# Three of sixteen states of a selective scan get their input product on GpSimd, and TensorE adds the skip term

## The chip, the cores and the metric

The kernel runs on one core of one Trainium2 chip. The metric is the device time of one execution in microseconds. The engines are TensorE (PE, matmuls), VectorE (DVE), ScalarE (ACT), GpSimd (POOL) and SyncE (SP, here only DMAs). Each takes its own instructions in the order in which they are written, and they meet through semaphores.

## The reference

Four layers run one after the other on x of 2 x 2048 x 128: an RWKV block, a feed-forward block of ternary weights, a selective state-space layer and a mixture of eight experts. The change touches only the state-space layer. For a batch row, with inner width 256 and 16 states, it computes

```
h, gate = split(xn @ W_in);  h = silu(causal_conv(h));  gate = silu(gate)
ts, Bm, Cm = split(h @ W_x);  dt = softplus(ts @ W_dt + b_dt)
state[t] = exp(dt[t] * -exp(A_log)) * state[t-1] + dt[t] * h[t] * Bm[t]     (256 x 16 states)
y[t] = sum over the 16 states of state[t] * Cm[t]   +   D * h[t]
out = layer_norm((y * gate) @ W_out);   x = x + out
```

The code folds a layer norm in front of this layer into `xn`.

## The kernel before, in words

The stage is `phase_ssm`. Channels lie on the 128 partitions, so the width 256 makes CB = 2 chunks, and time lies along the free dimension in tiles of N = 512 columns. Two batch rows by NT = 4 stretches of time give eight tiles, taken one after the other; the text calls them the first to the eighth (or last). The tiles of t = 1 and t = 2 are the third to the sixth. A tile works through DST = 16 states, numbered n = 0 to 15, and `body` of each engine is written as a loop over n.

For a state n:

- TensorE broadcasts the row of B over the partitions (L990, into a bank of `pD`) and the row of C (L993, into `pC`).
- ScalarE copies C to SBUF (`csb`, L1103) and computes the decay exp(dt * A) of the next state for both chunks (`dA`, L1092).
- VectorE multiplies `dtu` = dt * h with the broadcast of B. This product is called dBu. For an odd n it is two instructions (L1252, L1253), for an even n one of 1024 columns (L1255). Its result lies in `pD` in PSUM. Then it runs the recurrence with one TENSOR_TENSOR_SCAN for each chunk (L1240).
- GpSimd multiplies the scanned state with C for both chunks (`prod`, L1177) and keeps the last column as carry (L1168).
- TensorE sums the products of all states with an identity matrix in `pY` (`accumulate`, L979), LAG = 3 states behind: in iteration n it takes state n-3, and in n = 0, 1, 2 the last three states of the tile before.

`dA`, `hs`, `csb` and `prod` are rings of four slots.

Into this loop the work of the neighbouring tiles is written. `prep` prepares the next tile: TensorE has a step of it in each iteration n = 0 to 9 (centring, variance, four convolution steps L931 in n = 2 to 5, gate projection L938 in n = 6, the projections to ts, B and C L945 in n = 7 and 8, dt L952 in n = 9). ScalarE has its steps in n = 0, 1, 4, 5, 6, 8, 9, 10 and 11 (L1051 parks the convolution in n = 4 and 5; in n = 6 come two table loads, the silu of h and of the gate; L1062 and L1065 copy ts and `split` in n = 8). VectorE has xn in n = 1 (L1208), L1212, L1216 and L1219 in n = 8, 9 and 10. `tail` finishes the tile before: VectorE adds D * h to `pY` in n = 2 (L1225) and frees `pY` with it, GpSimd multiplies with the gate (L1160), TensorE projects down in n = 11 and takes a variance in n = 13. The first product of a tile, `accumulate(t, b, 0)` in n = 3, has to wait until that VectorE tail has read `pY`. ScalarE and GpSimd also split two pieces of expert weights in each of the first six tiles, which SyncE loads into two buffers `raw`.

## Time and profile before

| | us |
|---|---|
| median of 3 runs (lowest, highest) | 1486.36 (1486.03, 1488.72) |
| the profiled execution, its own time | 1486.03 |
| its span, first to last instruction | 1483.9 |
| mean granted clock of TensorE | 0.905 of full speed |

The scan stage fills the slices 17 to 31 of the 40 on the page. The page gives busy time in tenths of each slice, and the clock that TensorE was granted:

```profile
PE   4444279969789698797978888797866837978864
DVE  3676544644644453389999999999998286755644
ACT  2555343442443433575858677685743623544544
POOL 0111232230330220268788787878776246777773
PEclk8677589989999998999999999999999957999995
```

VectorE is at 9 tenths through the stage, the others at 6 to 9.

In a timeline row the first number is the start in us from the span's start and the second the duration of the whole group (xCOUNT). Matmuls in f32 of 512 columns are recorded as two MATMULs each, so a pair over two chunks is x4. PE ends are modelled and overlap the next start; the distance of two starts is the rate. What stands in brackets is the engine's idle time before the row and what ended it.

### The profile page before, as it was taken

How to read it: one execution, taken by the hardware profiler on the slowest of the kernel's cores; microseconds unless marked ns; L12 is line 12 of the kernel's file. 1: busy time of each engine (PE TensorE's matmuls, PEld its weight loads, DVE VectorE, ACT ScalarE, POOL GpSimd, SP SyncE). 2: the span in 40 equal slices, each digit the busy share in tenths (PEclk: the TensorE clock that was granted, in tenths of full speed). 3: DMA queues.
4: the chain of work that ended last, by engine and by line, in shares of the span. 5: the costliest groups of instructions: out<-in, count | busy, mean ns of one | idle time of the engine just before them, and what ended most of it. 6: DMA issues, size and time to landing. Idle time of an engine off the chain costs nothing. (4 is left out here: it accounts for less than half of the span.)

```text
span 1483.9 us, 16813 instructions
## 1 busy us (share of the span) xinstructions
PE 1110.5 (75%) x4986; PEld 549.9 (37%) x4986; DVE 1008.9 (68%) x1422; ACT 767.9 (52%) x1248; POOL 738.6 (50%) x615
## 2 busy tenths in 40 slices
PE   4444279969789698797978888797866837978864
PEld 1111123424334244232333333333322425967753
DVE  3676544644644453389999999999998286755644
ACT  2555343442443433575858677685743623544544
POOL 0111232230330220268788787878776246777773
PEclk8677589989999998999999999999999957999995
DMA  6000000000000000000000000000000001111124
GB/s 200 0 0 0 0 0 1 1 1 1 0 0 0 0 0 29 0 29 0 29 0 29 14 15 17 12 0 0 0 1 0 29 29 37 50 51 50 50 50 169
DMA packets 13842, 33.17 MB, mean 22 GB/s; under 512 B 3568, under 2 KB 3760, under 8 KB 13552
## 3 DMA queue, kind: packets, MB, share of 16 engines
q1 hardware_dynamic: 8784, 22.10, 4.5%
q0 software_dynamic: 4992, 10.23, 2.4%
q8 instruction: 36, 0.59, 0.2%
q14 instruction: 30, 0.25, 0.1%
HBM read 23.01 MB, written 9.31 MB: 22 GB/s over the span
## 5 line engine op out<-in xcount | busy, mean ns | idle before, releaser
L1177 POOL TENSOR_TENSOR prod<-hs,csb 128x1024 f32<-128x1024 f32 x128 | 303.9, 2375 | 117.7 <-DVE hs L1240 115.2
L1240 DVE TENSOR_TENSOR_SCAN hs<-dA,carry,pD 128x512 f32<-128x512 f32 x256 | 313.8, 1267 | 5.5 <-DVE pD L1255 0.8
L979 PE MATMUL pY<-prod,const 128*128 128x512 f32 x512 | 244.8, 600 | 11.6 <-DVE h L1225 7.4
L1092 ACT ACTIVATE dA<-dt,negA 128x512 f32<-128x512 f32 x256 | 169.3, 712 | 2.5 <-POOL dt L1149 2.5
L1103 ACT ACTIVATE csb<-pC 128x512 f32<-128x512 f32 x128 | 76.2, 595 | 154.8 <-PE pC L993 154.6
L979 PEld LDWEIGHTS pY<-prod,const 128*128 128x128 f32 x512 | 95.3, 190 | 120.9 <-issue 98.5
L645 ACT ACTIVATE stage<-pR,vec 128x512 f32<-128x512 f32 x64 | 44.0, 687 | 123.7 <-PE pR L481 123.7
L1914 DVE SCALAR_TENSOR_TENSOR hid<-pR,silu 128x512 f32<-128x512 f32 x78 | 53.9, 691 | 65.7 <-ACT silu L1646 65.6
L1699 POOL DMA_INDIRECT g<-moe_rows,source x78 | 81.9, 1050 | 26.9 <-issue 23.2
L1255 DVE TENSOR_TENSOR pD<-dtu,pD 128x1024 f32<-128x1024 f32 x64 | 78.5, 1227 | 22.6 <-POOL dtu L1153 9.9
L1715 POOL DMA_INDIRECT moe_outs<-y,to x78 | 80.9, 1038 | 23.8 <-issue 23.2
L990 PE MATMUL pD<-split,sel 96*128 96x512 bf16 x128 | 50.2, 392 | 54.1 <-DVE hs L1240 54.1
L1646 ACT ACTIVATE silu<-pR 128x512 f32<-128x512 f32 x78 | 46.6, 597 | 81.5 <-PE pR L1439 81.5
L1437 PE MATMUL pR<-x,moe_hi 128*128 128x256 f16 x312 | 87.3, 280 | 0.9 <-DVE x L1898 0.9
L1438 PE MATMUL pR<-x,moe_hi 128*128 128x256 f16 x312 | 87.2, 279 | 0.0
L1439 PE MATMUL pR<-x,moe_lo 128*128 128x256 f16 x312 | 87.0, 279 | 0.0
L666 POOL TENSOR_TENSOR mix_lo<-mix,mix_hi 128x512 f16<-128x512 f32 x8 | 9.5, 1210 | 152.3 <-DVE mix_hi L730 152.3
L931 PE MATMUL pQ<-xn,convw 128*128 128x512 f32 x128 | 67.2, 654 | 17.9 <-DVE xn L1208 17.8
L301 POOL TENSOR_TENSOR o<-o,rs 128x512 f32<-128x512 f32 x8 | 11.7, 1464 | 136.1 <-DVE o L394 136.1
L705 DVE TENSOR_SCALAR B_hi<-stage 128x512 f16<-128x512 f32 x64 | 36.9, 582 | 51.9 <-ACT stage L645 51.9
L705 DVE TENSOR_SCALAR A_hi<-stage 128x512 f16<-128x512 f32 x64 | 28.0, 442 | 46.0 <-ACT stage L645 46.0
L1545 PE MATMUL pY<-moe_hi,hid_hi 128*128 x312 | 57.3, 221 | 0.8 <-DVE hid_lo L1905 0.8
(342 smaller groups left out, 2776.1 us busy)
## 6 DMA issues: line engine op xcount, KB each, us to landing
raw<-moe_w SPq DMA_DIRECT2D x12, 512.0 KB, 3.6
room<-moe_outs SPq DMA_DIRECT2D x8, 512.0 KB, 8.5
X<-xT SPq DMA_DIRECT2D x4, 512.0 KB, 4.5
hidw<-hid_w SPq DMA_DIRECT2D x1, 2048.0 KB, 10.1
moe_rows<-xt SPq DMA_DIRECT2D x8, 256.0 KB, 2.0
outT<-X SPq DMA_DIRECT2D x8, 256.0 KB, 2.0
g<-moe_rows,source POOLq DMA_INDIRECT x78, 2.8
moe_outs<-y,to POOLq DMA_INDIRECT x78, 2.5
```

The lines of the kernel that those rows point to most:

```text
L931: last = nc.tensor.matmul(Q[c][:], convw[:, c, k, :], xn[:, b, k:k + N], start=k == 0, stop=k == TAPS - 1)
L979: last = nc.tensor.matmul(YB[c][:], G.ident, prod[:, slot(b, n), c, :], start=n == 0, stop=n == DST - 1)
L1092: last = nc.scalar.activation(dA[:, slot(b, n), c, :], dt[:, b, c, :], ACT.Exp, scale=negA[:, c, n:n + 1])
L1103: nc.scalar.activation(csb[:, slot(b, n), 0, :], CC[:], ACT.Copy).then_inc(S["c_in"], 1)
L1177: nc.gpsimd.tensor_tensor(prod[:, slot(b, n), :, :], hs[:, slot(b, n), :, :], csb[:, slot(b, n), :, :].to_broadcast([P, CB, N]), ALU.mult)\
L1240: last = nc.vector.tensor_tensor_scan(hs[:, slot(b, n), c, :], dA[:, slot(b, n), c, :], dBu(n, c), carry[:, b, n, c:c + 1], ALU.mult, ALU.add)
L1255: last = nc.vector.tensor_tensor(DD[:, 0:CB, :], dtu[:, b, :, :], bcastB(n).unsqueeze(1).to_broadcast([P, CB, N]), ALU.mult)
L1437: nc.tensor.matmul(out, w_hi, x_hi, start=start, stop=False)
L1438: nc.tensor.matmul(out, w_hi, x_lo, start=False, stop=False)
L1439: return nc.tensor.matmul(out, w_lo, x_hi, start=False, stop=stop)
L1699: nc.gpsimd.indirect_dma_start(g[:, i % GR, r, :], None, rows, bass.IndirectOffsetOnAxis(ap=source[:, 2 * i + r:2 * i + r + 1], axis=0))\
L1715: nc.gpsimd.indirect_dma_start(outs, bass.IndirectOffsetOnAxis(ap=to[:, 2 * i + r:2 * i + r + 1], axis=0), y[:, i % YR, r, :], None).then_ ...
```

## The change

HELPED names the states 3, 5 and 9. For these, VectorE no longer makes dBu. Three iterations ahead (LEAD), TensorE broadcasts their row of B into `pC` behind the broadcast of C, ScalarE copies it to SBUF (`bsb`), and GpSimd multiplies `dtu` with it into `helped` (two buffers). Their decay goes to the banks of `pD` in PSUM that their dBu would have filled (`decay_helped`); the half in the first bank waits until the scan of the state before has read it (`scan0`). Their scans take chunk 1 first.

D * h is added by TensorE, with a diagonal matrix of D, into the sum in `pY` in n = 10; VectorE's tail then multiplies the sum with the gate itself, and GpSimd's gate multiplication is gone.

On TensorE, the broadcast of B for state n+1 stands in iteration n, behind `accumulate(n-3)` and ahead of `prep`; before it stood at the head of iteration n+1. With it, `accumulate` has moved ahead of `prep`.

To make room in SBUF, `raw` and `scaled` have one buffer instead of two. The core of the diff:

```
+    HELPED = (3, 5, 9)
+    OWN = tuple(n for n in range(DST) if n not in HELPED)
+    LEAD = 3
...
+        bsb = sb("bsb3", [P, 1, N])
+
+        diagD = G.win[:, 0:INTER].rearrange("p (c m) -> p c m", c=CB)
+        helped = sb("helped3", [P, 2, CB, N])
         prod = sb("prod3", [P, RING, CB, N])
...
-        raw = sb("raw3", [P, 2, 2 * FFN])
+        raw = sb("raw3", [P, 2 * FFN])
...
+        def before_helped(n):
+
+            i = HELPED.index(n)
+            return HELPED[i - 2] + 1 if i >= 2 else HELPED[i - 2] + 1 - DST
...
-                if i >= 2:
-                    sp.wait_ge(S["w_low"], i - 1)
-                sp.dma_start(raw[:, i % 2, :], G.moe_w13[:, i, :] if i < E else w2[:, i - E, :])\
-                  .then_inc(S[f"w_in{i % 2}"], 16)
+                if i >= 1:
+                    sp.wait_ge(S["w_low"], i)
+                sp.dma_start(raw[:, :], G.moe_w13[:, i, :] if i < E else w2[:, i - E, :])\
+                  .then_inc(S["w_in"], 16)
...
-                    wait_past(pe, S["y"], chunk(t, b, 0) - 1)
+                    wait_past(pe, S["ygated"], at(t, b) - 1)
...
+            def broadcast_b(t, b, n):
+                wait_past(pe, S["scan"], state(t, b, n) - 2)
+                nc.tensor.matmul(bcastB(n), G.sel[:, n, :], split[:, b, :], start=True, stop=True)\
+                  .then_inc(S["bcastB"], 1)
+
             def body(t, b):
                 for n in range(DST):
 
                     if n == 0:
                         pe.wait_ge(S["split3"], at(t, b))
                         pe.wait_ge(S["split4"], at(t, b))
-                    wait_past(pe, S["scan"], state(t, b, n) - 2)
-                    nc.tensor.matmul(bcastB(n), G.sel[:, n, :], split[:, b, :], start=True, stop=True)\
-                      .then_inc(S["bcastB"], 1)
+                        broadcast_b(t, b, 0)
                     wait_past(pe, S["c_in"], state(t, b, n) - 1)
+                    if n - 1 + LEAD in HELPED:
+                        pe.wait_ge(S["b_in"], among(t, b, n - 1 + LEAD, HELPED))
                     nc.tensor.matmul(CC[:], G.sel[:, DST + n, :], split[:, b, :],
                                      start=True, stop=True).then_inc(S["bcastC"], 1)
+                    if n + LEAD in HELPED:
+                        pe.wait_ge(S["c_in"], state(t, b, n))
+                        nc.tensor.matmul(CC[:], G.sel[:, n + LEAD, :], split[:, b, :], start=True, stop=True)\
+                          .then_inc(S["bcastH"], 1)
                     if n < LAG and not is_first(t, b):
                         accumulate(*before(t, b), DST - LAG + n)
+                    if n >= LAG:
+                        accumulate(t, b, n - LAG)
+                    if n + 1 in OWN:
+                        broadcast_b(t, b, n + 1)
                     if not is_last(t, b) and n in PE_PREP:
                         prep(*after(t, b), PE_PREP.index(n))
                     if not is_first(t, b) and n in PE_TAIL:
                         tail(*before(t, b), PE_TAIL.index(n))
-                    if n >= LAG:
-                        accumulate(t, b, n - LAG)
+                    if n == 10:
+                        for c in range(CB):
+                            nc.tensor.matmul(YB[c][:], diagD[:, c, :], h[:, b, c, :], start=False, stop=False)
...
+            pe.wait_ge(S["diagD"], 1)
...
+            def decay_helped(t, b, n):
+                act.wait_ge(S["scan"], state(t, b, n) - 2)
+                nc.scalar.activation(dBu(n, 1), dt[:, b, 1, :], ACT.Exp, scale=negA[:, 1, n:n + 1])
+                act.wait_ge(S["scan0"], among(t, b, n, HELPED))
+                nc.scalar.activation(dBu(n, 0), dt[:, b, 0, :], ACT.Exp, scale=negA[:, 0, n:n + 1])\
+                  .then_inc(S["dA"], 1)
+
             def body(t, b):
                 for n in range(DST):
                     if n == 0:
                         act.wait_ge(S["dt"], at(t, b))
                         decay(t, b, 0)
+                    if n in HELPED:
+                        decay_helped(t, b, n)
                     act.wait_ge(S["bcastC"], state(t, b, n))
                     wait_past(act, S["prod"], slot_before(t, b, n))
                     nc.scalar.activation(csb[:, slot(b, n), 0, :], CC[:], ACT.Copy).then_inc(S["c_in"], 1)
-                    if n + 1 < DST:
+                    if n + LEAD in HELPED:
+                        act.wait_ge(S["bcastH"], among(t, b, n + LEAD, HELPED))
+                        wait_past(act, S["dBuH"], among(t, b, n + LEAD, HELPED) - 1)
+                        nc.scalar.activation(bsb[:, 0, :], CC[:], ACT.Copy).then_inc(S["b_in"], 1)
+                    if n + 1 in OWN:
...
-                    pool.wait_ge(S["y"], chunk(t, b, CB - 1))
-                    wait_past(pool, S["down"], at(t, b) - 1)
-                    nc.gpsimd.tensor_tensor(ygate[:, :, :], h[:, b, :, :], sgate[:, b, :, :], ALU.mult)\
-                      .then_inc(S["ygated"], 1)
-                elif step == 1:
                     pool.wait_ge(S["scaledC"], at(t, b))
-                    nc.gpsimd.tensor_tensor(X[:, b, ds(t)], X[:, b, ds(t)], scaled[:, b, :], ALU.add)\
+                    nc.gpsimd.tensor_tensor(X[:, b, ds(t)], X[:, b, ds(t)], scaled[:, :], ALU.add)\
...
+                    if n + LEAD in HELPED:
+                        k = among(t, b, n + LEAD, HELPED)
+                        pool.wait_ge(S["b_in"], k)
+                        wait_past(pool, S["scan"], state(t, b, 0) - 1 + before_helped(n + LEAD))
+                        nc.gpsimd.tensor_tensor(helped[:, HELPED.index(n + LEAD) % 2, :, :], dtu[:, b, :, :],
+                                                bsb[:, :, :].to_broadcast([P, CB, N]), ALU.mult)\
+                          .then_inc(S["dBuH"], 1)
                     if not is_last(t, b) and n in (10, 11, 12):
                         prep(*after(t, b), (10, 11, 12).index(n))
-                    if not is_first(t, b) and n in (2, 15):
-                        tail(*before(t, b), (2, 15).index(n))
+                    if not is_first(t, b) and n == 15:
+                        tail(*before(t, b), 0)
...
             def tail(t, b, step):
                 if step == 0:
                     dve.wait_ge(S["acc"], state(t, b, DST - 1))
+                    wait_past(dve, S["down"], at(t, b) - 1)
                     for c in range(CB):
-                        nc.vector.scalar_tensor_tensor(out=h[:, b, c, :], in0=h[:, b, c, :], scalar=col("D", c),
-                                                       in1=YB[c][:], op0=ALU.mult, op1=ALU.add).then_inc(S["y"], 1)
+                        last = nc.vector.tensor_tensor(ygate[:, c, :], YB[c][:], sgate[:, b, c, :], ALU.mult)
+                    last.then_inc(S["ygated"], 1)
                 elif step == 1:
                     dve.wait_ge(S["rstdC"], at(t, b))
-                    wait_past(dve, S["addedC"], at(t, b) - B)
-                    nc.vector.tensor_tensor(scaled[:, b, :], Q[0][:], rstd[:, b, :], ALU.mult)\
+                    wait_past(dve, S["addedC"], at(t, b) - 1)
+                    nc.vector.tensor_tensor(scaled[:, :], Q[0][:], rstd[:, b, :], ALU.mult)\
                       .then_inc(S["scaledC"], 1)
...
             def scan(t, b, n):
-                dve.wait_ge(S["dBu"], state(t, b, n))
-                dve.wait_ge(S["dA"], state(t, b, n))
-
                 wait_past(dve, S["prod"], slot_before(t, b, n))
                 wait_past(dve, S["kept"], slot_before(t, b, n))
-                for c in range(CB):
-                    last = nc.vector.tensor_tensor_scan(hs[:, slot(b, n), c, :], dA[:, slot(b, n), c, :],
-                                                        dBu(n, c), carry[:, b, n, c:c + 1],
-                                                        ALU.mult, ALU.add)
+                dve.wait_ge(S["dA"], state(t, b, n))
+                if n in OWN:
+                    dve.wait_ge(S["dBu"], among(t, b, n, OWN))
+                    for c in range(CB):
+                        last = nc.vector.tensor_tensor_scan(hs[:, slot(b, n), c, :], dA[:, slot(b, n), c, :],
+                                                            dBu(n, c), carry[:, b, n, c:c + 1],
+                                                            ALU.mult, ALU.add)
+                        if c == 0 and n + 1 in HELPED:
+                            last.then_inc(S["scan0"], 1)
+                else:
+                    dve.wait_ge(S["dBuH"], among(t, b, n, HELPED))
+                    for c in (1, 0):
+                        last = nc.vector.tensor_tensor_scan(hs[:, slot(b, n), c, :], dBu(n, c),
+                                                            helped[:, HELPED.index(n) % 2, c, :],
+                                                            carry[:, b, n, c:c + 1], ALU.mult, ALU.add)
                 last.then_inc(S["scan"], 1)
 
             def body(t, b):
                 for n in range(DST):
                     if n == 0:
                         dve.wait_ge(S["dtu"], at(t, b))
-                    dve.wait_ge(S["bcastB"], state(t, b, n))
-                    wait_past(dve, S["scan"], state(t, b, n) - 1)
-                    if n % 2:
+                    if n in HELPED:
+                        pass
+                    elif n % 2:
+                        dve.wait_ge(S["bcastB"], among(t, b, n, OWN))
+                        wait_past(dve, S["scan"], state(t, b, n) - 1)
                         nc.vector.tensor_tensor(dBu(n, 0), dtu[:, b, 0, :], bcastB(n), ALU.mult)
-                        last = nc.vector.tensor_tensor(dBu(n, 1), dtu[:, b, 1, :], bcastB(n), ALU.mult)
+                        nc.vector.tensor_tensor(dBu(n, 1), dtu[:, b, 1, :], bcastB(n), ALU.mult).then_inc(S["dBu"], 1)
                     else:
-                        last = nc.vector.tensor_tensor(DD[:, 0:CB, :], dtu[:, b, :, :],
-                                                       bcastB(n).unsqueeze(1).to_broadcast([P, CB, N]), ALU.mult)
-                    last.then_inc(S["dBu"], 1)
+                        dve.wait_ge(S["bcastB"], among(t, b, n, OWN))
+                        wait_past(dve, S["scan"], state(t, b, n) - 1)
+                        nc.vector.tensor_tensor(DD[:, 0:CB, :], dtu[:, b, :, :],
+                                                bcastB(n).unsqueeze(1).to_broadcast([P, CB, N]), ALU.mult)\
+                          .then_inc(S["dBu"], 1)
...
+            dve.wait_ge(S["turned"], 1)
+            for c in range(CB):
+                last = nc.vector.tensor_scalar(diagD[:, c, :], G.ident, col("D", c), None, ALU.mult)
+            last.then_inc(S["diagD"], 1)
```

TensorE from iteration n = 3 on in a middle tile, before (L990 B, L993 C, L931 convolution for the next tile, L979 sum):

```order
L990 MATMUL pD<-split,sel 128x512
L993 MATMUL pC<-split,sel 128x512
L931 MATMUL pQ_0<-xn,convw 128x512 x2
L979 MATMUL pY_0<-prod,const 128x512
L979 MATMUL pY_1<-prod,const 128x512
L990 MATMUL pD<-split,sel 128x512
L993 MATMUL pC<-split,sel 128x512
L931 MATMUL pQ_1<-xn,convw 128x512 x2
L979 MATMUL pY_0<-prod,const 128x512
L979 MATMUL pY_1<-prod,const 128x512
```

And in the changed kernel from the same place (L1014 C, L995 sum, L1001 B of the next state, L947 convolution):

```order
L1014 MATMUL pC<-split,sel 128x512
L995 MATMUL pY_0<-prod,const 128x512
L995 MATMUL pY_1<-prod,const 128x512
L1001 MATMUL pD<-split,sel 128x512
L947 MATMUL pQ_0<-xn,convw 128x512 x2
L1014 MATMUL pC<-split,sel 128x512
L995 MATMUL pY_0<-prod,const 128x512
L995 MATMUL pY_1<-prod,const 128x512
L947 MATMUL pQ_1<-xn,convw 128x512 x2
L1014 MATMUL pC<-split,sel 128x512
L995 MATMUL pY_0<-prod,const 128x512
L995 MATMUL pY_1<-prod,const 128x512
```

The convolution of iteration 3 stood ahead of the first sum of the tile and now stands behind it; iterations 4 and 5 have lost or moved their broadcast of B.

TensorE in iteration n = 6 of the changed kernel (L1018 is the broadcast of B for a helped state, L954 the gate projection):

```order
L1014 MATMUL pC<-split,sel 128x512
L1018 MATMUL pC<-split,sel 128x512
L995 MATMUL pY_0<-prod,const 128x512
L995 MATMUL pY_1<-prod,const 128x512
L1001 MATMUL pD<-split,sel 128x512
L954 MATMUL pQ_0<-xn,ssmw 128x512
L954 MATMUL pQ_1<-xn,ssmw 128x512
```

Two broadcasts now go to the one tile `pC` in a row; between them lies ScalarE's copy of the first.

ScalarE in iterations 8 and 9, before (L1103 csb, L1092 decays, L1062 ts, L1065 split):

```order
L1103 ACTIVATE csb<-pC 128x512
L1092 ACTIVATE dA<-dt,negA 128x512 x2
L1062 ACTIVATE tsb<-pQ_0 64x512
L1065 ACTIVATE split<-pQ_1 96x512
L1103 ACTIVATE csb<-pC 128x512
L1092 ACTIVATE dA<-dt,negA 128x512 x2
```

And in the changed kernel (L1144 csb, L1093 ts, L1096 split, L1130 and L1132 the decay of helped state 9, L1124 decays of state 10):

```order
L1144 ACTIVATE csb<-pC 128x512
L1093 ACTIVATE tsb<-pQ_0 64x512
L1096 ACTIVATE split<-pQ_1 96x512
L1130 ACTIVATE pD<-dt,negA 128x512
L1132 ACTIVATE pD<-dt,negA 128x512
L1144 ACTIVATE csb<-pC 128x512
L1124 ACTIVATE dA<-dt,negA 128x512 x2
```

The decays of state 9 stood ahead of the copies of ts and split, and now stand behind them.

## Rows read from the trace of the kernel before

**Rows 1.** The page, costliest groups: busy us, mean ns, idle before

```profile
L1177 POOL TENSOR_TENSOR prod<-hs,csb 128x1024 f32<-128x1024 f32 x128 | 303.9, 2375 | 117.7 <-DVE hs L1240 115.2
...
L1240 DVE TENSOR_TENSOR_SCAN hs<-dA,carry,pD 128x512 f32<-128x512 f32 x256 | 313.8, 1267 | 5.5 <-DVE pD L1255 0.8
...
L979 PE MATMUL pY<-prod,const 128*128 128x512 f32 x512 | 244.8, 600 | 11.6 <-DVE h L1225 7.4
```

**Rows 2.** Busy time by stretch, tail to tail, six middle tiles

```profile
core 0: us, PE busy (x) PEld busy (x) DVE busy (x) ACT busy (x) POOL busy (x), PEclk, DMA share, GB/s
...
765.06:830.34 65.28, 54.92 (x139) 22.13 (x138) 63.09 (x65) 46.89 (x74) 53.38 (x39) 1.00 0.05 17
...
sum 393.68, PE 330.30 PEld 131.79 DVE 377.72 ACT 276.94 POOL 315.94; mean PE 55.05 PEld 21.97 DVE 62.95 ACT 46.16 POOL 52.66
```

**Rows 3.** Waits of VectorE there: us, times, longest

```profile
DVE pD L1255 <- PE pD L990: 5.3, 7, 1.2
```

**Rows 4.** Timeline, VectorE, third tile: start us, us

```profile
762.69 2.45 DVE L1240 TENSOR_TENSOR_SCAN hs<-dA,carry,pD 128x512 f32<-128x512 f32 x2 [0.19 <-DVE pD L1255]
765.06 1.38 DVE L1225 SCALAR_TENSOR_TENSOR h<-h,vec,pY 128x512 f32<-128x512 f32 x2
...
774.05 0.70 DVE L1252 TENSOR_TENSOR pD<-dtu,pD 128x512 f32<-128x512 f32 x1
...
775.38 2.45 DVE L1240 TENSOR_TENSOR_SCAN hs<-dA,carry,pD 128x512 f32<-128x512 f32 x2
777.94 1.23 DVE L1255 TENSOR_TENSOR pD<-dtu,pD 128x1024 f32<-128x1024 f32 x1
...
794.02 0.76 DVE L1216 CAST mid<-sq 96x512 bf16<-96x512 f32 x1
```

**Rows 5.** Timeline, TensorE in the third tile

```profile
763.68 1.88 PE L931 MATMUL pQ<-xn,convw 128*128 128x512 f32 x4
...
766.58 1.96 PE L979 MATMUL pY<-prod,const 128*128 128x512 f32 x4 [1.02 <-DVE h L1225]
768.37 0.38 PE L990 MATMUL pD<-split,sel 96*128 96x512 bf16 x1
768.59 0.38 PE L993 MATMUL pC<-split,sel 96*128 96x512 bf16 x1
768.81 1.88 PE L931 MATMUL pQ<-xn,convw 128*128 128x512 f32 x4
770.53 1.88 PE L979 MATMUL pY<-prod,const 128*128 128x512 f32 x4
...
786.13 1.88 PE L945 MATMUL pQ<-h,ssmw 128*96 128x512 f32 x4
```

**Rows 6.** Timeline, ScalarE in the third tile

```profile
769.01 0.60 ACT L1103 ACTIVATE csb<-pC 128x512 f32<-128x512 f32 x1 [3.32 <-PE pC L993]
769.50 1.32 ACT L1092 ACTIVATE dA<-dt,negA 128x512 f32<-128x512 f32 x2
...
789.00 0.58 ACT L1065 ACTIVATE split<-pQ 96x512 bf16<-96x512 f32 x1
```

**Rows 7.** Timeline, TensorE in other tiles, after waiting

```profile
695.22 3.66 PE L931 MATMUL pQ<-xn,convw 128*128 128x512 f32 x4 [2.35 <-DVE xn L1208]
...
1024.17 1.99 PE L931 MATMUL pQ<-xn,convw 128*128 128x512 f32 x4 [2.34 <-DVE xn L1208]
...
1093.91 3.75 PE L979 MATMUL pY<-prod,const 128*128 128x512 f32 x4 [4.60 <-DVE h L1225]
```

**Rows 8.** Timeline, TensorE and VectorE in the first tile

```profile
632.91 0.63 PE L993 MATMUL pC<-split,sel 96*128 96x512 bf16 x1
...
662.72 0.75 DVE L1216 CAST mid<-sq 96x512 bf16<-96x512 f32 x1
```

**Rows 9.** Timeline, the end of the stage

```profile
1150.61 2.34 POOL L1160 TENSOR_TENSOR ygate<-h,sgate 128x1024 f32<-128x1024 f32 x1 [2.21 <-DVE h L1225]
...
1153.10 1.95 PE L960 MATMUL pQ<-ygate,ssmw 128*128 128x512 f32 x4 [1.84 <-POOL ygate L1160]
```

24 lines of the change are left out of this document (13 added, 11 removed).

## The prediction

> **What bounds the kernel now.** I read the page first, for where the change lies and what is full there. VectorE is busiest in the scan stage; its largest group is the scans, 256 of 1267 ns, almost without idle time before them, while GpSimd's products wait for those scans for 115.2 us [rows 1]. Then the busy time from tail to tail (start of the L1225 pair) of the six middle tiles: a tile takes 65.6 us (393.68 / 6), in which VectorE is busy 62.95, GpSimd 52.7, ScalarE 46.2 and TensorE 55.1 [rows 2]. Taken over a tile, VectorE is the bound and its instructions are what to remove. The waits say that it isn't the bound everywhere: its dBu waits for a broadcast of B on TensorE 5.3 us in six tiles, 0.88 a tile [rows 3]. So the next view is the order of time, the three engines side by side in the third tile.
>
> There a full f32 pair over both chunks goes every 1.72 us and a bf16 broadcast takes 0.22 (768.81 to 770.53, 768.37 to 768.59) [rows 5]. In n = 3 to 9 TensorE has two broadcasts, a pair of sums and a step of preparation, 0.44 + 1.72 + 1.72 = 3.88 us a state. VectorE needs 3.89 for an odd state (774.05 to 777.94) [rows 4]. The two are equally slow in this half of the tile. In the other half TensorE has no large preparation, and VectorE alone sets the pace. A faster VectorE in n = 3 to 9 therefore finds TensorE in front of it. And all three helped states lie in 3 to 9.
>
> **The change part by part**, laid out on the clock of the third tile.
>
> VectorE. A helped state loses its dBu, 774.05 to 775.38 = 1.33 us, and the 0.1 us that the next dBu waits after a scan (2.56 to the next start against 2.37 from 762.69 to 765.06) partly returns [rows 4]: 1.43 a state, 4.3 a tile. With the 0.88 us of waits gone too this would be 5.2. The tail has two multiplications instead of the two fused ones, 0.1 us shorter.
>
> TensorE. Three broadcasts go from B to the helped row, none is saved. The two matmuls with D add 1.72 us in n = 10, where TensorE has waited for VectorE before: nothing. The order is what counts. Before, the convolution step of n = 3 (763.68) ran while TensorE waited for `pY` to be freed; after it, it waited only 1.02 us more, to 766.58 [rows 5]. Now the first sum stands ahead of the convolution, so the wait is some 2.9 us with nothing in it, and the 1.72 us come behind it. The wait itself ends at 766.48, because VectorE's tail in n = 2 is where it was. From there TensorE has a chain without a gap:
>
> - n = 3: sum 1.79 (766.58 to 768.37), B 0.22, convolution 1.72: 3.73
> - n = 4: C 0.22, sum 1.72, convolution 1.72: 3.66
> - n = 5: C, sum, B, convolution: 3.88
> - n = 6: C, then the helped row. It goes to the same `pC`, so it waits until ScalarE has copied C: the parking of the convolution first (0.6), then csb, 0.60 long and 0.42 behind C's start at best (769.01 against 768.59) [rows 5, 6], and 0.14 to wake TensorE as at 766.44 to 766.58. That makes 1.51 instead of 0.22. Then 0.22 + 1.72 + 0.22 + 1.72: 5.39
> - n = 7: 3.88. Its projection needs the gate from ScalarE, for which TensorE waited in the old order; the new one arrives later and I find no wait left
> - n = 8: C, sum, projection to B and C with its end: 3.82
>
> The sum is 24.36 us, so that projection ends at 790.84. Before, it started at 786.13 and ended at 788.01 [rows 5]. Now state 9 hangs on it: ScalarE copies `split` first (0.5 with the start) and only then makes the two decays of state 9 (1.32, and 0.05 to VectorE) [rows 6], which stood ahead of that copy before and now stand behind it. Then come the scans, 2.37. State 9 is scanned at 790.84 + 0.5 + 1.37 + 2.37 = 795.08. The old one was done at 794.02, where L1216 starts [rows 4]. From tail to there it is 30.02 us now against 28.96, and since the six tiles waited 0.88 on average and this one 0.58 [rows 3], against 29.26 on average: +0.76 a tile. Behind state 9 both kernels are bound by VectorE with the same instructions. The stalls lie where the saved 4.3 us were: dBu of 7 waits for its B, the scan of 8 for ScalarE, the scan of 9 for its decay. ScalarE reaches the copy of split at about the same time by its own queue (two table loads, the silus, a piece of weights), 0.1 us ahead; what it loses comes on top. Middle tiles: 6 x 0.76 = +4.6.
>
> GpSimd. Three products more of about 2.37 (the form of `prod` has 2375 ns) [rows 1], one less (L1160, 2.34) [rows 9]: 53.4 + 4.8 = 58.2 us busy in a tile of 66. The one for state 9 is issued behind `prod` of 6 and needed some 8 us later. Nothing. The decay into PSUM and the scans with their operands exchanged have no row here; I take them as their SBUF forms (1.32 for the pair, 2.37), with 10% either way as bounds, 0.13 on ScalarE and 0.24 on VectorE in the chain, 6 x 0.37 = 2.2 us. The helped round trip of n = 6 is bounded by 0.22 (no wait) and 2.5 (ScalarE behind by another pair): -7.7 to +6 over six tiles. One wait is new without being on the path: in n = 2 ScalarE copies the helped row of 5 to the one `bsb` only when GpSimd has made the product of 3, some 5 us behind the scan of 0 (2.37 for `prod`, 2.37 for the product, the carry between). Queued behind it are a piece of weights and the decays of 3, and by my times these are ready 1 us before VectorE's tail ends. The single `raw` is loaded in the time between two splits, tens of us for a 3.6 us transfer on the page: nothing.
>
> First tile: no tail there, so the chain starts behind C of n = 3 (632.91 + 0.43, TensorE at half clock there) [rows 8]. With the sum at 2.02 it ends at 657.5, and state 9 at 661.7 against 662.72: -1.0. Last tile: no preparation, so states 5 and 9 save their 1.43 each; state 3 saves nothing, since B of 4 stays behind the sum, slow there (3.75) [rows 7]: -2.8. End: GpSimd's gate multiplication lay on the path, 1150.61 to 1153.10: -2.45 with 0.04 for the wake [rows 9]. Start: two small diagonal matrices in front of the first matmuls, +0.4.
>
> Sum without the clock: 4.6 - 1.0 - 2.8 - 2.45 + 0.4 = -1.3 us.
>
> **The clock.** TensorE falls from 2.4 to 1.2 GHz in some tiles after it has waited: the convolution behind a wait of 2.35 took 3.66 us in one tile and 1.99 behind 2.34 in another, and behind 4.60 the sum took 3.75 [rows 7]. A fall costs 1.7 us. Of the six middle tiles it came in three, in a place where TensorE had time. Now there are 2.9 idle us just ahead of the chain. I take three falls again, this time on the chain: 3 x 1.7 = +5.1. The Trainium skill (TensorE: Matmul & The Clock Gate, "HAM oscillation - how this bites in real kernels") says that a wait between short bursts throttles the engine again at every burst. By it all six tiles would fall; the three that did not under the shorter wait speak against "every", and it is the fourth rival below.
>
> Forecast: 1486.0 (this execution) - 1.3 + 5.1 = 1489.8; the median of the runs lies 0.3 higher, so 1490.
>
> **The rivals.**
> - VectorE stays the bound (0.08). Then 5.2 a tile in seven tiles, the last and the end as above: -36 - 5.3 + 0.4, 1446. For it: VectorE is busy 96% of a tile. Against: 3.88 us a state on TensorE in n = 3 to 9.
> - The chain is shorter than I make it, by the round trip in n = 6 or by ScalarE (0.17): -7.7 - 1.3, about 1477.
> - No fall or one, else as forecast (0.20): 1485 to 1487.
> - The clock falls in every tile, or also in the first and last (0.17): 6 or 8 times 1.7, 1495 to 1499. This one is slower, by one thing: the bare wait for `pY`. It decides from the fourth tile on that falls.
> - ScalarE, not TensorE, is last at state 9 (0.08): it is 0.1 us ahead in my sum, and its wait for GpSimd to free `bsb` in n = 2 or a late csb in n = 6 moves everything behind; at 1.5 us a tile, 1499.
> - The forecast, two to four falls: 0.30; its own range is 1488 to 1492.
>
> About 0.2% (3 us) is what a measurement can tell from no change. Faster takes the first two: 0.25. Same takes the third and the lower edge of the forecast: 0.27. Slower: 0.48. The range 1475 to 1500 leaves out the first rival and the far ends of the last two.
>
> **What the new profile would show.** VectorE waits inside n = 4 to 9, by 4 us a tile or more, for `pD` from TensorE and from ScalarE; if it has no such waits, the first rival holds. TensorE idles nearly 3 us ahead of the first sum of a tile. Its helped broadcast in n = 6 starts 1.5 us behind C. From the start of the tail to the end of the scan of state 9 it is 30 us, or 31.7 where the first sum takes 3.4. The last tile is shorter by 3 us, the end by 2.5. I am wrong at the root if a middle tile takes under 63 us.

## The result and the profile after

The changed kernel takes 1503.74 us (median of 4 runs, 1502.13 to 1504.87), the kernel before 1486.28 (4 runs on the same chip, 1486.03 to 1488.72): a ratio of 1.0113, interval 1.0095 to 1.0130. It is slower, as forecast, by 17.5 us where 4 were forecast, and outside the range. The profiled execution took 1502.13 us, its span is 1500.3 against 1483.9.

First the page of the kernel after, the costliest groups of the scan stage (line, engine, operation, names, shapes, count, then busy us, mean ns of one, and idle us before them with what ended most of it).

```profile
L1217 POOL TENSOR_TENSOR prod<-hs,csb 128x1024 f32<-128x1024 f32 x128 | 302.8, 2366 | 95.7 <-DVE hs L1287 73.2
L995 PE MATMUL pY<-prod,const 128*128 128x512 f32 x512 | 261.6, 635 | 21.4 <-DVE ygate L1272 17.5
L1287 DVE TENSOR_TENSOR_SCAN hs<-dA,carry,pD 128x512 f32<-128x512 f32 x208 | 254.9, 1267 | 20.6 <-ACT dA L1124 8.8
...
L1295 DVE TENSOR_TENSOR_SCAN hs<-pD,carry,helped 128x512 f32<-128x512 f32 x48 | 58.9, 1268 | 9.3 <-ACT pD L1132 4.4
```

In [rows 1] the scans had almost no idle time before them; now the own ones have 20.6 us and the helped ones 9.3. A scan with its operands exchanged takes 1268 ns, the same as any other. Next the busy time from tail to tail of the six middle tiles, the view of [rows 2] (a tail now starts with the L1272 pair):

```profile
core 0: us, PE busy (x) PEld busy (x) DVE busy (x) ACT busy (x) POOL busy (x), PEclk, DMA share, GB/s
...
769.96:837.64 67.68, 58.20 (x142) 23.16 (x142) 59.84 (x60) 48.56 (x77) 57.76 (x41) 0.97 0.06 16
...
sum 410.44, PE 351.24 PEld 139.88 DVE 357.64 ACT 283.40 POOL 342.38; mean PE 58.54 PEld 23.31 DVE 59.61 ACT 47.23 POOL 57.06
```

VectorE is busy 3.34 us less in a tile (59.61 against 62.95) and the tile is 2.79 us longer (410.44 / 6 = 68.41 against 65.61), so VectorE idles 8.8 us in a tile where it idled 2.7. What ends those idle times is in the waits of VectorE over the scan stage (us, times, longest):

```profile
DVE pD L1309 <- PE pD L1001: 10.6, 7, 1.5
DVE pD L1314 <- PE pD L1001: 10.4, 11, 1.6
...
DVE hs L1287 <- ACT dA L1124: 8.8, 7, 1.3
DVE sq L1258 <- ACT split L1096: 8.6, 7, 1.4
...
DVE hs L1295 <- ACT pD L1132: 4.4, 7, 1.0
```

The first two rows are `pD` from TensorE, 21.0 us. Over the six middle tiles alone, the stretch of [rows 3], they are 17.3 (9.1 and 8.2) where the kernel before had 5.3. Two others are new in kind: the own scan of state 8 waits for its decays, and L1258 (it subtracts `split` from the projection) for ScalarE's copy of the projection. In order of time, VectorE from the tail of the third tile (start us, duration, engine, line, in brackets the idle time before and its releaser), to be read beside [rows 4]:

```profile
769.96 1.26 DVE L1272 TENSOR_TENSOR ygate<-pY,sgate 128x512 f32<-128x512 f32 x2
...
786.42 0.70 DVE L1309 TENSOR_TENSOR pD<-dtu,pD 128x512 f32<-128x512 f32 x1 [1.53 <-PE pD L1001]
...
792.80 2.45 DVE L1287 TENSOR_TENSOR_SCAN hs<-dA,carry,pD 128x512 f32<-128x512 f32 x2 [1.20 <-ACT dA L1124]
796.53 0.69 DVE L1258 TENSOR_TENSOR sq<-pQ,split 96x512 f32<-96x512 f32 x1 [1.28 <-ACT split L1096]
797.81 2.46 DVE L1295 TENSOR_TENSOR_SCAN hs<-pD,carry,helped 128x512 f32<-128x512 f32 x2 [0.59 <-POOL carry L1208]
```

And TensorE over the same stretch, beside [rows 5]:

```profile
771.37 1.95 PE L995 MATMUL pY<-prod,const 128*128 128x512 f32 x4 [1.77 <-DVE ygate L1272]
773.16 0.38 PE L1001 MATMUL pD<-split,sel 96*128 96x512 bf16 x1
773.38 1.88 PE L947 MATMUL pQ<-xn,convw 128*128 128x512 f32 x4
...
782.62 0.38 PE L1014 MATMUL pC<-split,sel 96*128 96x512 bf16 x1
784.05 0.39 PE L1018 MATMUL pC<-split,sel 96*128 96x512 bf16 x1 [1.05 <-ACT csb L1144]
...
793.99 1.88 PE L961 MATMUL pQ<-h,ssmw 128*96 128x512 f32 x4
```

The sum stands in front and the engine waits for the tail. Then TensorE is not idle for 24.5 us (771.37 to 795.87, where the projection of L961 ends) but for the exchange over `pC` in n = 6, 1.43 us from C to the helped row. The helped broadcasts, B and the sums follow one another as the sum of the prediction had it.

Now the stage by its parts, each taken from the starts of the same instructions in both traces (end of scan 9: start of the cast behind it; last row: the rest of the span):

| part | before | after | change | forecast |
|---|---|---|---|---|
| first dBu to first tail | 78.03 | 79.26 | +1.23 | -1.0 |
| six tiles, tail to end of scan 9 | 175.27 | 186.54 | +11.27 | +9.7 |
| six tiles, end of scan 9 to next tail | 218.41 | 223.90 | +5.49 | 0 |
| last tile, tail to tail | 56.75 | 55.94 | -0.81 | -2.8 |
| last tail to end of the stage | 12.90 | 10.88 | -2.02 | -2.45 |
| ahead of and behind the stage | | | +1.2 | +0.4 |
| span | 1483.9 | 1500.3 | +16.4 | +3.8 |

### The profile page after: what moved, and what is told of

The parts are those of the page before. It is cut to its first block and busy times, and to the rows that moved or that the text cites. A ratio compares the mean times of both kernels' runs of the same rounds, so it can differ in the third digit from the quotient of the medians.

```text
span 1500.3 us, 16996 instructions
## 1 busy us (share of the span) xinstructions
PE 1139.6 (76%) x5018; PEld 560.7 (37%) x5018; DVE 981.8 (65%) x1376; ACT 779.1 (52%) x1272; POOL 774.4 (52%) x631
## 5 line engine op out<-in xcount | busy, mean ns | idle before, releaser
L995 PE MATMUL pY<-prod,const 128*128 128x512 f32 x512 | 261.6, 635 | 21.4 <-DVE ygate L1272 17.5
L1287 DVE TENSOR_TENSOR_SCAN hs<-dA,carry,pD 128x512 f32<-128x512 f32 x208 | 254.9, 1267 | 20.6 <-ACT dA L1124 8.8
L995 PEld LDWEIGHTS pY<-prod,const 128*128 128x128 f32 x512 | 102.1, 202 | 123.1 <-issue 110.8
L1124 ACT ACTIVATE dA<-dt,negA 128x512 f32<-128x512 f32 x208 | 138.1, 716 | 2.5 <-POOL dt L1194 2.5
L1144 ACT ACTIVATE csb<-pC 128x512 f32<-128x512 f32 x128 | 75.7, 591 | 81.9 <-PE pC L1014 81.7
L1778 POOL DMA_INDIRECT moe_outs<-y,to x78 | 84.2, 1080 | 23.8 <-issue 23.5
L1001 PE MATMUL pD<-split,sel 96*128 96x512 bf16 x104 | 40.7, 391 | 36.1 <-DVE hs L1287 35.9
L1295 DVE TENSOR_TENSOR_SCAN hs<-pD,carry,helped 128x512 f32<-128x512 f32 x48 | 58.9, 1268 | 9.3 <-ACT pD L1132 4.4
L947 PE MATMUL pQ<-xn,convw 128*128 128x512 f32 x128 | 62.5, 615 | 2.0 <-DVE xn L1254 1.9
```

What stands on the lines that cost most here:

```text
L947: last = nc.tensor.matmul(Q[c][:], convw[:, c, k, :], xn[:, b, k:k + N], start=k == 0, stop=k == TAPS - 1)
L995: last = nc.tensor.matmul(YB[c][:], G.ident, prod[:, slot(b, n), c, :], start=n == 0, stop=n == DST - 1)
L1124: last = nc.scalar.activation(dA[:, slot(b, n), c, :], dt[:, b, c, :], ACT.Exp, scale=negA[:, c, n:n + 1])
L1144: nc.scalar.activation(csb[:, slot(b, n), 0, :], CC[:], ACT.Copy).then_inc(S["c_in"], 1)
L1287: last = nc.vector.tensor_tensor_scan(hs[:, slot(b, n), c, :], dA[:, slot(b, n), c, :], dBu(n, c), carry[:, b, n, c:c + 1], ALU.mult, ALU.add)
L1778: nc.gpsimd.indirect_dma_start(outs, bass.IndirectOffsetOnAxis(ap=to[:, 2 * i + r:2 * i + r + 1], axis=0), y[:, i % YR, r, :], None).then_ ...
```

## The experiments

They ran on other chips of the same kind than the first comparison. There the kernel before takes 1540 to 1548 us (its medians). Nearly all of the extra time lies behind the scan stage: 56.6 of the 59.2 us by which the trace of `control` (below) is longer than the first one of the same kernel. Ratios are always to the kernel before on the same chip; the scan stage (first dBu to its end, 541.36 us before and 556.52 after) is compared as it stands, since the unchanged kernel after took 556.37 in it there (`control`, below). Stage times are of one execution each. "Six tiles" means tail to tail of the middle tiles, 393.68 before and 410.44 after.

**conv_first.** The convolution step of n = 3 goes back in front of the sum that waits for the tail.

```diff
+                    if n == LAG and not is_last(t, b):
+                        prep(*after(t, b), PE_PREP.index(n))
                     if n >= LAG:
                         accumulate(t, b, n - LAG)
...
-                    if not is_last(t, b) and n in PE_PREP:
+                    if not is_last(t, b) and n in PE_PREP and n != LAG:
```

> The changed kernel with one edit: in n = 3 TensorE does the convolution step ahead of the first sum of the tile, as before the change; the broadcast of B stays behind the sum. Theory A (a chain on TensorE from the freed pY to the scan of state 9): the 1.72 us of convolution go back into the wait, 6 x 1.72 = 10.3 us less, and the shorter wait lets the clock fall in fewer places, up to 5 us more: 1489 to 1494. Rival B (ScalarE's own queue is last at state 9, it was only 0.1 us ahead in the sum): then little is won, within 3 us of 1503.7.

Measured: ratio 1.0008 (0.9994 to 1.0022), stage 539.91, six tiles 395.25. Tail to end of scan 9 is 28.5 to 28.6 us in all six tiles, against 30.22 in the unfallen tiles of the kernel after: 1.7 less, the length of the convolution step, in every tile. And no middle tile falls to the lower clock there. TensorE in the third tile of this kernel:

```profile
767.83 1.88 PE L947 MATMUL pQ<-xn,convw 128*128 128x512 f32 x4
769.73 1.95 PE L995 MATMUL pY<-prod,const 128*128 128x512 f32 x4
```

The convolution lies in the wait again. 410.44 - 395.25 = 15.2 us are returned; 6 x 1.72 + 3 x 1.7 = 15.4. The chain on TensorE is shown to be what sets state 9, and this one place in the order, with the falls that its wait brings, is worth nearly the whole loss: the stage is 16.6 us shorter than after and 1.5 shorter than before.

**h_behind.** The helped row is issued behind the sum instead of directly behind C, so that its wait for ScalarE is covered by the sum.

```diff
-                    if n + LEAD in HELPED:
-                        pe.wait_ge(S["c_in"], state(t, b, n))
-                        nc.tensor.matmul(CC[:], G.sel[:, n + LEAD, :], split[:, b, :], start=True, stop=True)\
-                          .then_inc(S["bcastH"], 1)
...
                         accumulate(t, b, n - LAG)
+                    if n + LEAD in HELPED:
+                        pe.wait_ge(S["c_in"], state(t, b, n))
+                        nc.tensor.matmul(CC[:], G.sel[:, n + LEAD, :], split[:, b, :], start=True, stop=True)\
+                          .then_inc(S["bcastH"], 1)
```

> The changed kernel with one edit: the broadcast of B for a helped state stands behind the sum of the same iteration instead of ahead of it, so TensorE doesn't wait for ScalarE's copy of C with nothing to do. Theory A (only TensorE's chain counts): n = 6 is 1.3 us shorter, 6 x 1.3 = 7.8 us less: 1496. Rival B (ScalarE in its own order is as late as TensorE): its copy of the helped row, and all behind it in n = 6 (decays, table loads, silus), comes some 0.5 us later or more, TensorE then waits for the gates in n = 7, and the time is 1503 to 1508.

Measured: ratio 1.0119 (1.0101 to 1.0138), stage 558.84, six tiles 412.28: not better, 2.3 us worse than the kernel after. The tiles that don't fall take 30.32 to 30.38 us from tail to the end of scan 9, against 30.23 to 30.31 in the kernel after, so nothing was won on the path; of the 2.3 us, 1.5 lie in the seventh tile, which fell for longer (33.37), and 1.1 at the end. The round trip of n = 6 was on TensorE's chain, but taking it away there moves it to ScalarE, which makes the decays of the states behind later, and TensorE waits in n = 7 for the gate, as rival B had it. A row of TensorE in the seventh tile, and waits of VectorE in this kernel:

```profile
1068.12 1.90 PE L961 MATMUL pQ<-h,ssmw 128*64 128x512 f32 x4 [1.25 <-ACT sgate L1089]
```

```profile
DVE hs L1287 <- ACT dA L1124: 21.7, 14, 2.7
...
DVE hs L1295 <- ACT pD L1132: 9.6, 14, 1.7
```

In the kernel after these waits were 8.8 and 4.4 us, and that row had no wait. TensorE and ScalarE are thus equally late here, as the fifth rival had them within 0.1 us.

**filler.** Ten matmuls on a constant, each of 512 columns, stand in the wait of n = 3, ahead of C and the sum; their output is overwritten.

```diff
+                    if n == LAG:
+                        keep_busy(10)
```

> The changed kernel with one edit: in n = 3 TensorE does ten matmuls of 512 columns whose result nobody reads (2.2 us at 2.4 GHz), ahead of the broadcast of C, in the time in which it waits for pY. Theory A: the falls to 1.2 GHz on the first sum (three of six middle tiles took 31.9 us from tail to the end of the scan of 9, the others 30.2) follow from the idle time, so they vanish, and 3 x 1.7 = 5 us go, 1498 to 1499. Rival B: the falls don't depend on this wait but on TensorE's load over the tile, and the time stays within 2 us of 1503.7.

Measured: ratio 1.0100 (1.0080 to 1.0120), stage 552.46, six tiles 405.85. The falls at the first sum are gone: tail to scan 9 is 30.2 to 30.6 in all six. TensorE in the fourth tile, and below it the same tile of the kernel after, where it fell:

```profile
838.71 2.32 PE L987 MATMUL pC<-sel 96*128 96x512 bf16 x10
...
841.09 1.88 PE L995 MATMUL pY<-prod,const 128*128 128x512 f32 x4
```

```profile
839.05 3.59 PE L995 MATMUL pY<-prod,const 128*128 128x512 f32 x4 [2.76 <-DVE ygate L1272]
```

The sum takes 1.88 us behind the filler and 3.59 behind an idle 2.76. Three falls cost 410.44 - 405.85 = 4.6 us, 5.1 forecast. The filler costs something elsewhere: from the first dBu to the first tail it takes 81.44 us against 79.26. The run shows that the falls go when the wait is filled. It doesn't show that the wait alone makes them, since two_helped (below) has no fall in its middle tiles either, and its waits are unfilled.

**wait_order.** VectorE's waits ahead of a scan stood with dBu, the one that is met last, at the end. It is put first, behind it the decay, then the two for free buffers.

```diff
+                if n in OWN:
+                    dve.wait_ge(S["dBu"], among(t, b, n, OWN))
+                dve.wait_ge(S["dA"], state(t, b, n))
                 wait_past(dve, S["prod"], slot_before(t, b, n))
                 wait_past(dve, S["kept"], slot_before(t, b, n))
-                dve.wait_ge(S["dA"], state(t, b, n))
-                if n in OWN:
-                    dve.wait_ge(S["dBu"], among(t, b, n, OWN))
```

> The changed kernel with one edit: in front of a scan of a state that VectorE prepares itself, the wait for dBu stands first again, ahead of those for dA, prod and kept. Theory A: the gap from a dBu to its own scan grew from 1.26-1.27 to 1.33-1.37 us start to start because the last wait in the row is now the one that is released last. Then the gap is 1.27 again, the part of a tile in which VectorE sets the pace is 0.07 to 0.10 us a state shorter, over nine such states in seven tiles and thirteen in the last some 5 to 7 us: 1497 to 1499. Rival B: the gap comes from the scan's own operands or from the second set of counters, then it stays at 1.33-1.37 and the time at 1503.7 within 1.5 us.

**one_counter.** The same order, and dBu is counted over all 16 states (a helped state's scan adds its one), so that its threshold is the one that the other waits use (32 a step of time) and not 26. ScalarE's wait on the same counter is changed to match.

```diff
-                    dve.wait_ge(S["dBu"], among(t, b, n, OWN))
+                    dve.wait_ge(S["dBu"], state(t, b, n))
...
+                        if c == 1:
+                            last.then_inc(S["dBu"], 1)
```

> The changed kernel, with the wait for dBu first as in wait_order, and with dBu counting all states again (a helped state's first scan adds its one), so that its threshold is the same number as that for dA. In wait_order the gap from dBu to its scan was 1.27 us in the tiles with constant thresholds and 1.44 in the tiles of the loop. Theory A: the gap comes from thresholds that VectorE's sequencer works out between the waits; with one number for both it is 1.27 in all tiles, and the stage is about 556.5 - 5 to 6 us = 551. Rival B: it comes from the wait itself being on another semaphore; then the loop tiles stay at 1.33 to 1.45.

Measured: wait_order 1.0075 (1.0058 to 1.0091), stage 553.31; one_counter 1.0078 (1.0061 to 1.0095), stage 549.23, six tiles 406.88. What to read is the step from the start of a dBu to the start of its scan. First the kernel after, then wait_order, then one_counter, each in a tile in which t is a register of the loop:

```profile
824.64 1.23 DVE L1314 TENSOR_TENSOR pD<-dtu,pD 128x1024 f32<-128x1024 f32 x1
825.97 2.45 DVE L1287 TENSOR_TENSOR_SCAN hs<-dA,carry,pD 128x512 f32<-128x512 f32 x2
```

```profile
822.84 1.23 DVE L1315 TENSOR_TENSOR pD<-dtu,pD 128x1024 f32<-128x1024 f32 x1
824.29 2.45 DVE L1288 TENSOR_TENSOR_SCAN hs<-dA,carry,pD 128x512 f32<-128x512 f32 x2 [0.22 <-DVE pD L1315]
```

```profile
824.28 1.23 DVE L1317 TENSOR_TENSOR pD<-dtu,pD 128x1024 f32<-128x1024 f32 x1
825.54 2.45 DVE L1288 TENSOR_TENSOR_SCAN hs<-dA,carry,pD 128x512 f32<-128x512 f32 x2
```

1.33, 1.45 and 1.26; the kernel before has 1.26. In the tiles with a constant t the kernel after has mostly 1.35 or 1.36, wait_order mostly 1.25 to 1.27. So there are two costs. The wait for dBu at the end of the row costs 0.1 where all thresholds are constants and 0.07 in the loop; and in the loop, other thresholds behind that wait cost more, 0.19. The trace of wait_order shows what lies there: the register instruction for the threshold of the next wait (L1283) starts at 824.11, behind the end of the dBu at 824.07. In the kernel after and in one_counter the last one starts beside the dBu (824.75 and 824.31). With one threshold for all it costs nothing against the kernel before in either. Putting the last wait first therefore only helped where it also had no arithmetic behind it.

wait_order is 1.1 us shorter than the kernel after in the six tiles only because it has one fall in them and not three: behind state 9 it is 2.4 longer. one_counter has three falls, and behind state 9 it is 3.2 shorter. The whole executions don't show the difference between the two (1.0075 and 1.0078); the reading rests on the traces.

**halo_act.** The copy of three columns of `xn` (L1252) goes to ScalarE.

```diff
-                        nc.vector.tensor_copy(xn[:, b, 0:TAPS - 1], xn[:, b, N:N + TAPS - 1]).then_inc(S["halo"], 1)
...
+                        nc.scalar.activation(xn[:, b, 0:TAPS - 1], xn[:, b, N:N + TAPS - 1], ACT.Copy)\
+                          .then_inc(S["halo"], 1)
```

> The changed kernel with one edit: the three-column copy of xn in n = 1 (L1252), which took 1.0 us on VectorE against 0.14 before, is done by ScalarE behind its rstd. Theory A: on VectorE the copy is held up by GpSimd's product for helped state 3, which runs at that time; without it VectorE goes straight on to xn, 0.85 to 1.0 us less in each of six tiles: 1498 to 1499. Rival B: VectorE would wait there for something else anyway (rstd, the broadcast), then the wait moves to the instruction behind and the time stays within 1.5 us of 1503.7.

**two_helped.** `HELPED = (5, 9)`: state 3 is computed by VectorE again, so that GpSimd has no helped product in n = 1, where the copy is.

> The changed kernel with states 5 and 9 helped only, the three-column copy of xn left on VectorE. GpSimd then has no helped product in n = 0, and at the time of the copy it has just finished prod of state 0. Theory A (GpSimd's product holds up the copy): the copy takes 0.14 us again in all six places, against 0.98 to 1.05, and the first convolution of a tile comes that much earlier. Rival B (the copy is slow in the changed kernel for another reason, the new order of waits or the tiles' new places in SBUF): it stays at about 1 us.

Measured: halo_act 1.0065 (1.0045 to 1.0086), six tiles 403.47, 7.0 us less than after (5.5 of them behind state 9, 1.5 ahead of it, where two tiles fell and not three); two_helped 1.0029 (1.0017 to 1.0042), stage 545.58, six tiles 401.94. The copy over the stage in the kernel after, then in two_helped (smallest, median, largest ns, first and last start):

```profile
L1252 DVE COPY xn<-xn x6: 981/1009/1094, 695.0 to 1037.3; 128x3 f32<-128x3 f32 x6
```

```profile
L1252 DVE COPY xn<-xn x6: 141/142/145, 695.3 to 1030.3; 128x3 f32<-128x3 f32 x6
```

And what GpSimd does at that time in the kernel after, with the copy's own row:

```profile
830.94 2.34 POOL L1225 TENSOR_TENSOR helped<-dtu,bsb 128x1024 f32<-128x1024 f32 x1
...
832.29 1.01 DVE L1252 COPY xn<-xn 128x3 f32<-128x3 f32 x1
833.34 0.69 DVE L1254 TENSOR_TENSOR xn<-pQ,sq 128x512 f32<-128x512 f32 x1
```

The copy ends at 833.30, when the product has ended at 833.28. Without that product it takes 0.14 us, as before, where GpSimd was idle at that time. Shown: the helped product of state 3 holds the copy, 0.87 us a tile. By the Trainium skill (SBUF — State Buffer, "Who interferes with whom") a VectorE copy in a mode with two ports and a GpSimd operation exclude each other for the whole of the first one; the trace agrees, 0.14 against 1.01. That two_helped is faster than the kernel after by 10.9 us of stage, with one dBu more in every tile, says more: helping state 3 cost more than it gave. Of the six tiles' 8.5 us, 3.6 lie behind state 9 and 4.9 ahead of it, where no middle tile fell, though the sum waited 0.7 to 2.3 us.

**three.** conv_first, halo_act and wait_order together. **best1.** The same with one_counter.

> The edits of wait_order, halo_act and conv_first together in the changed kernel (states 3, 5 and 9 helped). Theory A: what they save lies in different places of a tile and adds up. The scan stage, from the first dBu to the first VectorE instruction of the next stage, was 541.4 us before, 556.5 changed, 539.9 with conv_first alone; with the other two (3.2 and some 6) it is about 531 to 533, 8 to 10 us under the kernel before, 1476 to 1479 where that has 1486. Rival B: VectorE, once faster in n = 10 to 2, meets the next wait (GpSimd, or the preparation), and the stage stays at 536 or more.

> one_counter, halo_act and conv_first together (states 3, 5 and 9 helped). three had these but for the counter, and its loop tiles took 66.2 us from tail to tail where its constant ones took 64.9. Theory A: all tiles take 64.9, six of them 388 instead of 393.3, the stage 531 instead of 536.1: 9 to 10 us under the kernel before, 0.3% under three. Rival B: within 1 us of three.

Measured: three 0.9977 (0.9967 to 0.9988), stage 536.06; best1 0.9939 (0.9924 to 0.9955), stage 528.47, six tiles 387.40. best1 beats both kernels: 12.9 us of stage under before, 28 under after. The parts were worth 15.2, 7.0 and 3.6 alone (six tiles), 25.8, and 23.0 together; the first two hold falls that can go only once. three came to rival B's time and not to that of Theory A; best1 came a little under what its Theory A said, 388 and 531.

**none_helped.** three with `HELPED = ()`: D by TensorE, the gate and the early B stay, VectorE computes all sixteen dBu.

> As three, but no state is helped: VectorE makes all sixteen dBu, so what is left of the change is D * h on TensorE, the gate on VectorE and the broadcast of B ahead of the preparation. Theory A (helping 3, 5 and 9 is worth nothing, TensorE sets n = 3 to 9): the same time as three within 3 us, stage 531 to 535. Rival B (the help does pay in part): 6 x 2 us and the last tile's 3 more, stage 542 to 548, 1487 to 1492.

Measured: 0.9982 (0.9972 to 0.9992), stage 536.39 against three's 536.06, as Theory A had it. The six tiles take 389.88, 3.4 us less than in three. Against best1, which has the same 1.26 us to a scan, helping three states gains 389.88 - 387.40 = 2.5 us in six tiles: 0.4 of the 4.3 us a tile that VectorE is relieved of. In the last tile, where TensorE has no preparation, it gains 4.6 (58.21 against 53.57), all of it. That is the prediction's view of n = 3 to 9, measured by itself: a lighter VectorE finds TensorE, and ScalarE with it (h_behind), in front of it.

**late3.** three with the helped states put where TensorE has no preparation, n = 11, 13, 15. One line is added besides: GpSimd waits for its own helped product ahead of the split in n = 10.

```diff
-    HELPED = (3, 5, 9)
+    HELPED = (11, 13, 15)
```

> As three, but the helped states are 11, 13 and 15 instead of 3, 5 and 9 (and GpSimd waits for its own helped product ahead of the split in n = 10). Theory A: a dBu taken off VectorE pays where VectorE alone sets the pace, n = 10 to 2, and not in n = 3 to 9 where TensorE is as slow: 4.3 us a tile less than a kernel with no state helped, stage 500 to 512, 1448 to 1458. Rival B: GpSimd, which has dt, dtu and the split in the same iterations, gets 7 us of products more there, is some 8 us late by n = 15 and holds VectorE through the ring of four: half or more is lost, stage 518 to 530, 1464 to 1475.

Measured: 1.0235 (1.0217 to 1.0253), stage 578.00. Far worse, and my theory that the place alone decides was wrong. The waits of TensorE and VectorE in the stage show what grew:

```profile
PE pC L1018 <- ACT csb L1150: 39.5, 24, 3.1
PE pY L995 <- POOL prod L1223: 28.9, 11, 4.7
...
DVE sq L1265 <- ACT split L1102: 26.7, 7, 6.0
```

24 helped rows wait 39.5 us for ScalarE to empty the one `pC`; in the kernel after the same 24 wait 28.3. The sums wait 28.9 for GpSimd's products where they waited 3.8, so GpSimd is late too, as rival B had it, by more than it said. Each exchange over the single buffer runs at ScalarE's pace, and the copy of the projection for which L1265 waits comes late on the same engine (26.7, in the kernel after 8.6). Which of these sets the time, and which of ScalarE's other work holds its two, I didn't take apart.

**mix and mix2.** best1 with `HELPED = (3, 5, 15)` and `(3, 15)`.

> best1 with the states 3, 5 and 15 helped instead of 3, 5 and 9. Theory A: state 9 as a helped one costs in n = 6 to 8 (TensorE waits for ScalarE's copy in n = 6, the decays of 9 wait for split), and state 15 lies where VectorE alone sets the pace, so its dBu pays 1.4 us. From tail to the scan of 9 it is 27.5 instead of 28.5, a tile 62.5 to 63.5, the stage 518 to 524. Rival B (late3 repeats itself): the exchange over the one pC in n = 12 meets ScalarE's own work, TensorE stands still there and state 15 loses more than it saves: stage 533 or more.

> best1 with only the states 3 and 15 helped. Theory A: a dBu of state 5 taken off VectorE is worth nothing, since TensorE sets the pace there: the same as mix within 2 us. Rival B: it pays as much as one of the other half, 1.4 us a tile: 8 us or more above mix.

Measured: mix 0.9959 (0.9944 to 0.9975), stage 534.66; mix2 0.9960 (0.9944 to 0.9975), 534.12. Both lose to best1 by 6 us. The two are alike, so over the stage the help for state 5 is worth nothing: it costs 2.2 us in the six tiles (392.16 against 390.00) and returns 1.5 in the last. And one helped state late in the tile is not better than one at 9.

**control.** The kernel after with nothing changed, on one of the experiments' chips.

> The changed kernel again, unchanged. If the stage is the same on this chip as on its first one, it takes 556 us within 2, with two to four of the six middle tiles at 31.9 us from tail to the scan of 9 and the others at 30.2, and the ratio to the kernel before is 1.010 to 1.013. If the place of the falls is fixed by the program and not by chance, it is again the second, fourth and seventh tile.

Measured: 1.0073 (1.0045 to 1.0101), stage 556.37, six tiles 410.37, falls in the second, fourth and seventh tile again. The stage repeats to 0.15 us, even in which tiles fall. The ratio is smaller than at first and than expected, 12 us instead of 17, while the stage is the same. Where the difference lies stays open, since no trace of the kernel before was taken on these chips; for the reading above, 3 to 5 us between a ratio and a stage time say nothing.

## Why the prediction was right and wrong

- **Right: which engine is next.** VectorE waits inside n = 4 to 9 for `pD` and for ScalarE, at the places named (states 4, 5, 6, 7, 8 and 9). The first rival (VectorE stays the bound, 1446) fell with that.
- **Right: the chain.** From the freed `pY` to the projection 24.5 us, 24.36 forecast; tail to the end of scan 9 30.22 in unfallen tiles, 30.02 forecast, and 31.85 to 32.00 in fallen ones, 31.7 forecast. conv_first took the first link out and got its 1.7 us back in every tile. 1.6 of the 12.6 us by which I was short are here.
- **Right: falls on the chain**, in three of the six middle tiles, at the first sum. filler shows that they go when the wait is filled, and their price: 4.6 us, 5.1 forecast. In conv_first and best1, where the convolution fills most of the wait and at most 1.07 us are left, no middle tile fell. That there were three again is luck: with the same order and waits up to 2.3, 2.2, 2.9 and 2.9 us there were none in two_helped, two in halo_act, one in wait_order and three in one_counter. The Trainium skill (TensorE: Matmul & The Clock Gate, "HAM oscillation - how this bites in real kernels") tells of a kernel that fell at every burst, with longer waits between its bursts than the 1.7 to 2.8 us here. In this kernel "every" does not hold: three tiles with the same order did not fall.
- **Wrong: "Behind state 9 both kernels are bound by VectorE with the same instructions."** This is the step that failed, 5.5 us. They are bound by VectorE there, and their instructions are the same, but they aren't as fast. I added up the steps from one start to the next over these six stretches in both traces. The copy of three columns takes 1.01 for 0.14 because a helped product runs beside it: +4.5, as five of the six copies lie here. The 54 steps from a dBu to its scan, nine a tile, are longer because dBu now has a counter of its own whose wait stands last: +3.3. The cast behind scan 9 is faster, 0.40 for [rows 4]'s 0.76: -2.1. The steps from a scan to the next dBu give -0.1, and with that the 5.5 are complete. Two runs take the causes out one by one: behind state 9 halo_act, without the copy, is 5.5 shorter, and one_counter 3.2. As to the cast, in the third tile of before GpSimd's piece of weights ran from 792.35 to 794.49 and the cast started in it, at 794.02; in that of after GpSimd was idle when it started (rows below). That this makes the difference is read from the rows alone; no run tests it. I had costed the helped products on GpSimd at "nothing" since the engine had room, and asked only for its time, not for what it holds up.
- **Wrong in size: the first tile**, +1.23 for -1.0. Up to scan 9 it gained half a microsecond; behind it the same causes cost 1.7.
- **Wrong in size: the last tile**, -0.8 for -2.8. Up to its last scan it gained 2.6 us (from the tail on 48.40 for 51.00), and with one counter it would have been 0.6 more (47.83 in one_counter). From there to the closing tail it lost 1.8, because the last sum ran at the lower clock, 3.78 us where the kernel before has 1.98; VectorE's wait of 6.29 us (rows below) holds that. one_counter, with neither, has 53.58 and best1 53.57, against 56.75 before: the savings were there.
- **End**: -2.0 for -2.45. The gate multiplication left GpSimd, and the projection starts 2.00 us behind the start of the tail instead of 3.97. It could have started sooner: ten matmuls that only keep TensorE busy (L987) stand ahead of it, and it starts when they are done, 0.7 us behind the end of the tail. I had left 0.04 for that. The rows of the end of the kernel after, answering to [rows 9]:

```profile
1162.88 3.78 PE L995 MATMUL pY<-prod,const 128*128 128x512 f32 x4 [1.78 <-POOL prod L1217]
...
1166.45 2.40 PE L987 MATMUL pC<-sel 96*128 96x512 bf16 x10
...
1166.69 1.29 DVE L1272 TENSOR_TENSOR ygate<-pY,sgate 128x512 f32<-128x512 f32 x2 [6.29 <-PE pY L995]
...
1168.69 1.88 PE L976 MATMUL pQ<-ygate,ssmw 128*128 128x512 f32 x4
```

- 0.9 us behind the stage are not explained.
- Of the bounds, those of the exchanged scans and the decay into PSUM weren't needed: a scan takes 1268 ns against 1267, a decay 686 against 716 for one into SBUF (means). The round trip of n = 6 was right (1.43 measured for 1.51), and so was it that ScalarE is only about 0.1 us ahead: h_behind gained nothing.

The rows for the cast, GpSimd's piece of weights in the kernel before (the cast's own row is in [rows 4]), then the product ahead of the cast, the cast, and GpSimd's next product in the kernel after:

```profile
792.35 2.14 POOL L1190 TENSOR_TENSOR moe_lo<-raw,moe_hi 128x1024 f32 x1
```

```profile
797.77 2.13 POOL L1237 TENSOR_TENSOR moe_lo<-raw,moe_hi 128x1024 f32 x1
...
800.18 0.40 DVE L1262 CAST mid<-sq 96x512 bf16<-96x512 f32 x1
...
800.35 2.45 POOL L1217 TENSOR_TENSOR prod<-hs,csb 128x1024 f32<-128x1024 f32 x1 [0.45 <-DVE hs L1295]
```


Together: 1.6 (chain) + 5.5 (behind state 9) + 2.2 (first tile) + 2.0 (last) + 0.4 (end) + 0.9 (behind the stage) = 12.6 us, the difference between 3.8 and 16.4.
